# Five traces of sequence 1 moved from the stretch in which sequence 0 runs ahead to the lone steps, in a fused four-layer kernel

## The reference

```python
# x: (16, 256, 256); every layer is added to its input
# layer 0: 16 gated exponential averages ("traces") over the tokens
gated  = x * sigmoid([x, ema(x)] @ Wg.T + bg)
mod    = 0.5 + sigmoid(gelu(x @ Wn1.T + bn1) @ Wn2.T + bn2)      # one factor per trace and token
traces = [ema_d(gated * mod[..., d]) for d in range(16)]
temporal = sum_d softmax(blend)[d] * traces[d]
out = (gelu(x @ Wsoma.T) * sigmoid(temporal @ Wtemp.T)) @ Wout.T ; layernorm
# layer 1: attention pooling with one score per token and one of three masks per sequence
# layer 2: eight gated experts (silu(h @ Wg[e]) * (h @ Wu[e])) @ Wd[e], weighted, plus a shared one
# layer 3: gelu(x @ W1 + b1) @ [W2 | We[index]]
```

## Time and profile before

| | us |
|---|---|
| median of 3 runs | 2922.68 (2922.46 to 2923.1) |
| the profiled execution | 2916.74 |
| its span | 2914.9 |
| TensorE busy | 2833.2 (97%) |
| VectorE busy | 1802.3 (62%) |
| ScalarE busy | 1429.1 (49%) |
| POOL busy | 1218.8 (42%) |
| mean granted TensorE clock | 0.988 of full |

### The profile page before, as it was taken

How to read it: one execution, slowest core, us unless ns; L and a number is a source line. 1 busy time by engine, 2 the same in 40 slices (tenths; PEclk the granted TensorE clock), 3 DMA queues, 4 the chain that set the end, 5 groups by cost and what they waited for, 6 DMA issues and landing times.

```text
span 2914.9 us, 37509 instructions
## 1 busy us (share of the span) xinstructions
PE 2833.2 (97%) x13486; PEld 2371.9 (81%) x13486; DVE 1802.3 (62%) x3018; ACT 1429.1 (49%) x2465; POOL 1218.8 (42%) x950
## 2 busy tenths in 40 slices
PE   4899999999999999999999999999999999999998
PEld 3688898888888888887888888888888888888887
DVE  7679778676665586566665567656565556334443
ACT  1345663574345553466334554357533447334544
POOL 4226346534543355433454335543444343333333
PEclk7899999999999999999999999999999999999999
DMA  2323231221111131112111112112111113111331
GB/s 102 103 91 96 89 102 49 66 87 55 50 53 46 44 98 45 48 45 93 44 44 48 51 48 83 48 47 66 62 50 54 48 53 95 54 44 53 116 98 39
DMA packets 76825, 189.81 MB, mean 65 GB/s; under 512 B 9176, under 2 KB 21984, under 8 KB 76640
## 3 DMA queue, kind: packets, MB, share of 16 engines
q1 hardware_dynamic: 73504, 178.91, 20.1%
q0 software_dynamic: 2560, 8.39, 0.9%
q10 hardware_dynamic: 576, 0.11, 0.0%
HBM read 183.18 MB, written 4.19 MB: 64 GB/s over the span
## 4 chain that ended last, share of the span: by engine, by line
PE 93%; DVE 4%; issue 1%; ACT 1%; POOL 0%; DMA 0%; DVEq 0%; SPq 0%; ACTq 0%; POOLq 0%
PE bank L514 20%; PE bank L516 20%; PE bank L515 20%; PE ps_out L514 9%; PE ps_out L516 9%; PE ps_out L515 9%; PE bank L507 3%; DVE trace L1011 1%; PE bank L584 1%; DVE trace L1003 1%; PE ps_out L669 1%; DVE w_lo L1080 1%; PE bank L632 0%; DVE acc L1135 0%; PE bank L618 0%
## 5 line engine op out<-in xcount | busy, mean ns | idle before, releaser
L1252 POOL TENSOR_TENSOR hid_lo<-hid,hid_hi 128x512 fp32r<-128x512 f32 (+1 forms) x640 | 852.8, 1333 | 1531.7 <-ACT hid_hi L895 1531.0
L514 PE MATMUL bank<-res_lo,w_hi 128*128 128x512 f32 (+1 forms) x2432 | 948.9, 390 | 4.7 <-issue 3.5
L516 PE MATMUL bank<-res_hi,w_hi 128*128 128x512 f32 (+1 forms) x2432 | 938.0, 386 | 0.0
L515 PE MATMUL bank<-res_hi,w_lo 128*128 128x512 f32 (+1 forms) x2432 | 937.9, 386 | 0.0
L1109 DVE TENSOR_TENSOR hid<-hid,bank 128x512 f32<-128x512 f32 (+1 forms) x608 | 398.8, 656 | 625.5 <-PE bank L516 509.1
L885 ACT ACTIVATE hid<-bank 128x512 f32<-128x512 f32 (+1 forms) x608 | 349.1, 574 | 715.1 <-PE bank L516 644.8
L1080 DVE TENSOR_TENSOR w_lo<-w_raw,w_hi 128x768 fp32r<-128x768 f32 (+1 forms) x488 | 446.0, 914 | 195.8 <-ACT w_hi L848 151.7
L516 PEld LDWEIGHTS bank<-res_hi,w_hi 128*128 128x128 f32 x2432 | 458.3, 188 | 96.8
L514 PEld LDWEIGHTS bank<-res_lo,w_hi 128*128 128x128 f32 x2432 | 458.3, 188 | 92.6 <-issue 5.7
L515 PEld LDWEIGHTS bank<-res_hi,w_lo 128*128 128x128 f32 x2432 | 458.8, 189 | 81.6
L848 ACT ACTIVATE w_hi<-w_raw 128x768 fp32r<-128x768 f32 x360 | 304.2, 845 | 437.5 <-PE ps_out L516 430.9
(11 more groups left out here) (180 smaller groups left out, 1930.5 us busy)
## 6 DMA issues: line engine op xcount, KB each, us to landing
w_raw<-in_chunks SPq DMA_DIRECT2D x360, 384.0 KB, 3.0
w_raw<-in_head_chunks SPq DMA_DIRECT2D x64, 224.0 KB, 2.5
plain<-in_chunks SPq DMA_DIRECT2D x32, 384.0 KB, 3.6
x_in<-in_xT SPq DMA_DIRECT2D x16, 256.0 KB, 3.5
out_yT<-acc SPq DMA_DIRECT2D x8, 512.0 KB, 2.8
acc<-in_sidew SPq DMA_DIRECT2D x2, 512.0 KB, 7.2
acc<-in_sidew SPq DMA_DIRECT2D x1, 320.0 KB, 5.6
trace<-in_penalties,pen_row POOLq DMA_INDIRECT x16, 3.6
```

The costliest lines, as they stand in the source:

```text
L514: mm(out, wh, xl, start=start and i == 0, stop=False, skip_group_check=not lone)
L515: mm(out, wl, xh, start=False, stop=False, skip_group_check=not lone)
L516: last = mm(out, wh, xh, start=False, stop=end, skip_group_check=not lone)
L1252: nc.gpsimd.tensor_tensor(hid_lo[i % DEPTH][:, tok], hid[i % 3][:, tok], f(hid_hi[i % DEPTH][:, tok]), ALU.subtract).then_inc(s_hlo, 1)
```

## The change

The table `fill` loses five pieces. The pieces 7 to 13 of sequence 1 of block 0 were in the lead stretch; now only 7 (behind piece 28 of sequence 0) and 8 (behind piece 40) are. `ahead` ends at 9 instead of 14, and the planner lays pieces 9 to 13 together with those that follow.

```diff
     first = [0, 2, 4, 5, 6, 7, 8, 3] + list(range(9, PIECES))
-    fill = {11: 1, 12: 1, 13: 1, 15: 1, 17: 1, 22: 2, 28: 2, 36: 1, 40: 1, 44: 1}
+    fill = {11: 1, 12: 1, 13: 1, 15: 1, 17: 1, 28: 1, 40: 1}
     ahead = 2
```

## The result

The changed kernel takes 2933.8 us (median of 6, 2931.55 to 2934.67) against 2922.57 for the one before, a ratio of 1.0041 with a 95% interval of 1.0028 to 1.0055; in a second comparison 2933.25 against 2919.39, 1.0049 (1.0035 to 1.0062). It is slower by 11 to 14 us. One of the six runs of the kernel before took 4764.76 us, counts in that median, and is left out of the ratio. The forecast was 2922.1, no change, with a range from 2918.5 to 2927.5: wrong. The profiled execution spans 2932.0 us, against the 2914.9 of the one before, so 17.1 is to be found in the two traces. That is more than the timed runs show, as the profile of before is of one of its quicker executions (2916.74, median 2922.57).

The account below looks back on a forecast made before the run. TensorE, busy 97% of the span, was taken as the bound, except in the lead stretch and lone steps. Lead -4.65 and lone steps and after +4.05 sum to -0.6: 2922.1 us against the median 2922.68, range 2918.5 to 2927.5.

Parts of the forecast that it names:

- Lead stretch: Before the first lone step: fewer traces ahead of two projections, 3.45 us saved plus 1.2 from the clock, sum -4.65.
- the clock's term: Output projection of the lead stretch: a shorter gap before it cuts 3.36 us to 2.15, 1.2 saved.
- Rival 1: Lead stretch gives back all VectorE loses, 10.9 us gained; total -6.8, 2915.8 us; chance 0.08.
- The loop in steps 9 to 14: Lone steps with added traces: TensorE idles in the loop from mix matmul to next trace, +3.9 us (bounds 1.5 and 7.0).
- rival 3: Clock falls once more in the lone steps: +1.2 us, 2923.3; chance 0.2.
- Later pieces move by two or three places at most, 0 with bounds of 1 either way: After the lone steps: side pieces shifted in the planner's list cost 0 us, within 1 either way.
- The closing of expert 1: Step 18: the closing is no longer late, so its wait of 0.48 us goes.
- The +0.9 at the probabilities: Pieces 42 and 44 come one step apart instead of two, so transposes of the probabilities wait for their product: +0.9 us.
- the wait of 1.1 at the closing in step 34: One less block 1 trace lies before this closing, so its wait goes: -0.9 us.
- rival 2: VectorE becomes the bound in steps 34 to 46: three traces, +6.5 us, total +5.9, 2928.6; chance 0.06.
- 6.5 for steps 34 to 46: Upper bound for VectorE's 16 traces instead of 13 there, each costing its 2.17 us; the prediction took 0.

Follow-up runs that it names:

- two_stretches: Changed kernel with side pieces behind steps 121 to 123 and 138 to 141 as in the kernel before; ratio to before 1.0030, median 2930.02 us.
- late_as_before: Changed kernel's order up to step 73, order of the kernel before from step 74 on; ratio to before 1.0022, median 2926.26 us.
- after_busy: Changed kernel plus 18 matmuls with unused results in TensorE's gaps of the lead stretch; ratio to before 1.0032, median 2926.88 us.
- late_as_after: Order of the kernel before up to step 73, changed kernel's order from step 74 on; ratio to before 1.0014, median 2925.06 us.
- after_again: The changed kernel run again unchanged; ratio to the kernel before 1.0049, median 2933.25 us.
- slots: Kernel before with all seven lead-stretch traces kept there, at places where VectorE is free; ratio to before 0.9993, median 2915.96 us.
- slots_fitted: slots plus matmuls with unused results, fitted to TensorE's gaps in lead stretch and lone steps; ratio to before 0.9970, median 2909.59 us.

## Why the prediction was wrong, point by point

- **Lead stretch: right, with luck in the clock's term.** The gate's projection came 1.07 earlier behind POOL's add (forecast 1.12), the output projection 3.44 (3.45), and it took 1.99 (2.15); the attention projection 4.81 (4.65). But two_stretches, with the same list there, ran the output projection at half clock and has its attention projection at 17.6 instead of 15.6, so the 1.2 of that term comes in some executions and not in others. Rival 1, that all of VectorE's 10.9 comes back, is refuted by the same rows.
- **The loop in steps 9 to 14: right**, to 0.1 us at each mix.
- **Clock: the step that failed first.** The clock was priced where it gave, the output projection, and not where it took. Pooling and first lone step were left as they were; they took 2.4 us more, as the rise came later in the shorter stretch. Of the lone steps rival 3 had one more fall for 1.2 and a chance of 0.2; there were two more by step 32, for 3.2 (the difference between after and late_as_before). Of the rule in the Trainium skill (TensorE: Matmul & The Clock Gate, section "HAM oscillation — how this bites in real kernels"), that waits between short bursts put the clock down again, the runs bear out more than was granted: after_busy regained 4.9 us by step 9 with nothing but matmuls in the gaps. Not as a fixed price for each step, though, since one list gave two clocks. The prediction's sum took a clock that one profile showed for a property of the list.
- **"Later pieces move by two or three places at most, 0 with bounds of 1 either way": the step that failed most.** It cost 7.3 us from step 74 to 142 in the profile, 0.14% in the timed runs of late_as_after. Waits from 400 to 700 us are 5.4 of it, and half clock behind two of them, of which before has one, is about the rest. The number of places says little; what counts is what a link of a chain meets when it has shifted. In steps 121 to 123 two links came to run beside POOL and took 3.05 us longer; in steps 138 to 141 TensorE had one step less to cover the probabilities.
- **Closings and probabilities, steps 15 to 32: wrong in part.** The closing of expert 1 was to lose its wait of 0.48 and has 0.97: pieces 3 and 4 of block 1 came to stand at steps 17 and 18, ScalarE loads tables for them, and SiLU and closing of that step are late. The +0.9 at the probabilities is right in size by luck: there is a wait of 1.01 in that step (175.63), but it is the mix of a trace of block 1 that waits for the scan of the trace before it, which stands one step ahead of it where it stood two; the transposes (178.44) wait for nothing. With the clock's 1.6 left out, the loss from step 9 to 32 is 6.2 (late_as_before), against 4.95 in the sum.
- **Steps 32 to 74:** the wait of 1.1 at the closing in step 34 went, as forecast, and VectorE did not become the bound (rival 2): at most 0.6 us of waits for it at one place. In all the stretch gave +1.5 instead of -0.9. TensorE's waits from 204 to 400 us add up to 2.5 before and 2.6 after: a closing waits 0.6, a plain fp32 projection (L507) 0.6 for VectorE's one_lo (L1025), a mix 0.3. The rest is not in waits, and I did not follow it to the end.
- **The range.** Its terms give 2919.4 to 2928.1 around the median, not the 2918.5 to 2927.5 that were stated, and they leave out two bounds that the text itself had named: 6.5 for steps 34 to 46 and 1 for the later pieces. With 3.8 for the clock and what goes with it up to step 9 (2.4 and 1.4), 1.6 for the fall near 190 and 7.3 for the late order, the forecast of -0.6 becomes about +12, of the +15.4 in the traces; the other 3.3 are the steps 9 to 32 (1.2) and 32 to 74 (2.4) above, less 0.3 elsewhere.

Open: what sets which of its two groups (2916 to 2918, 2921 to 2923) a run of before falls in. The slower group has the lower mean clock, but no profile of it was had. late_as_after gives a hint: its profile (2924.96) is of the upper one of its own two groups (2918.8 to 2921.6, 2924.9 to 2925.9), and on the list of before it lost 3.7 us by step 32 with two more half-clock stretches. late_as_before's (2922.36) is of the lower one of its groups (2921.1 to 2922.4, 2925.9 to 2927.6), and lacks two that after has. That such stretches make the upper group of before is not shown.

## What to carry to other kernels

Work that is hidden in one stretch has a price in the next; before moving it, look first for free places in the same stretch, which here gave the same 4.8 us at the attention projection without the loss behind it. Where a planner or a greedy list sets the order, treat each change of its input as a change of the whole list: compare the lists to the end, and look at every place where a chain's links have moved, what now stands ahead of them and what runs beside them on the other engines. Where the busiest engine idles in short gaps, price the clock on both sides of the gap, as a thing that differs between executions, and consider filling the gap.

## What the runs showed of the hardware

- One instruction list, three executions: step 32 at 162.8, 162.8 and 159.6 us; another list, 156.0, 156.7 and 159.7. Two more half-clock stretches are the difference in both, so one costs 1.5 to 1.9 us. Comparisons of single profiles on this kernel are good to some 4 us, no better.
- Matmuls with unused results made the kernel faster: 18 of them took the changed one from a ratio of 1.0049 to 1.0032 (after_again, after_busy), 41 took slots from 0.9993 to 0.9970 (slots_fitted). Both are 6.4 us by the medians, which come from different sets of runs.
- VectorE's TENSOR_SCALAR on 128x256 took 2.75 us for two, and 0.73 at another moment, with instructions of POOL running beside the slow ones; TENSOR_TENSOR with both inputs in SBUF (L1031) took 1.71 and 0.68. The product with an input in PSUM (L1109) took 0.68 at 569.92, though POOL's add of 569.41 ran beside it. The Trainium skill (GPSIMD Engine Reference, section "1. Specifications") says that GpSimd's SBUF interfaces are shared with VectorE, with contention where VectorE's instruction runs in a mode that uses two ports or has two inputs in SBUF; the trace agrees, at a price of nearly four times for the TENSOR_SCALAR.
